# Moving the tail of a Mamba block's softplus from VectorE to GpSimd, its positive part to ScalarE

## The reference

```
xc, z = split(x @ in_w.T)
u     = silu(causal_conv(xc))
dtx, Bm, Cm = split(u @ xproj_w.T)
dt    = softplus(dtx @ dt_w.T + dt_b)
dA    = exp(dt * A);   dBu = dt * Bm * u
h_t   = dA_t * h_(t-1) + dBu_t;   y_t = h_t . C_t
out   = ((y + u * D) * silu(z)) @ out_w.T
```

## Time and profile before

| what | value |
|---|---|
| median of 3 runs (lowest, highest) | 2064.76 us (2064.29, 2065.99) |
| the profiled execution's own time | 2069.39 us |
| its span in the trace | 2067.7 us |
| VectorE busy, share of span | 1474.6 us, 71% |
| GpSimd busy | 1046.0 us, 51% |
| ScalarE busy | 860.7 us, 42% |
| TensorE matmul busy | 1518.2 us, 73% |

### The profile page before, as it was taken

How to read it: one execution, slowest core, us unless ns; L and a number is a source line. 1 busy time by engine, 2 the same in 40 slices (tenths; PEclk the granted TensorE clock), 3 DMA queues, 4 the chain that set the end, 5 groups by cost and what they waited for, 6 DMA issues and landing times. The chain is left out here.

```text
span 2067.7 us, 19480 instructions
## 1 busy us (share of the span) xinstructions
PE 1518.2 (73%) x4666; PEld 860.3 (42%) x4667; DVE 1474.6 (71%) x1703; ACT 860.7 (42%) x1848; POOL 1046.0 (51%) x531
## 2 busy tenths in 40 slices
PE   6666776786677677667767766776710999999997
PEld 3233343443344344334434433443400566666665
DVE  3699999999999999999999999999730111211111
ACT  2554554645555464555546455555300222222221
POOL 2565675666557566655756665567335111121121
PEclk8778887898888789888878987898955999999999
DMA  6312303122130312213031221303078111111111
GB/s 183 146 47 77 139 23 119 47 101 79 56 142 25 113 53 95 82 52 142 26 113 52 96 82 52 122 24 112 0 231 243 19 25 24 23 25 25 23 25 19
DMA packets 64555, 159.31 MB, mean 77 GB/s; under 512 B 10702, under 2 KB 40508, under 8 KB 63708
## 3 DMA queue, kind: packets, MB, share of 16 engines
q1 hardware_dynamic: 52716, 145.17, 20.6%
q0 software_dynamic: 11760, 13.38, 4.0%
HBM read 137.17 MB, written 21.35 MB: 77 GB/s over the span
## 5 line engine op out<-in xcount | busy, mean ns | idle before, releaser
L630 POOL TENSOR_TENSOR ring<-dtu,brep 128x1536 f32<-128x1536 f32 x192 | 660.9, 3448 | 444.7 <-DVE states L641 352.3
L653 PE MATMUL py<-ring,ident 128*128 128x384 f32 x1536 | 645.2, 573 | 128.0 <-DVE yg L670 104.3
L641 DVE TENSOR_TENSOR_SCAN states<-states,ring 128x768 f32<-128x768 f32 x384 | 673.8, 1755 | 33.9 <-ACT states L617 18.9
L653 PEld LDWEIGHTS py<-ring,ident 128*128 128x128 f32 x1536 | 336.9, 226 | 423.1 <-issue 202.0
L617 ACT ACTIVATE states<-dt_,aneg 128x376 f32<-128x376 f32 x768 | 406.1, 560 | 0.0
L643 DVE TENSOR_TENSOR ring<-states,crep 128x768 f32<-128x768 f32 x384 | 367.4, 957 | 13.2
L1271 DVE TENSOR_TENSOR hid<-act_g,gu 128x768 f32<-128x768 f32 x55 | 52.5, 954 | 425.0 <-ACT act_g L1266 425.0
L614 ACT ACTIVATE states<-zero_cols 128x16 f32<-128x16 f32 x384 | 71.3, 186 | 643.8 <-DVE ring L643 638.7
L1260 PE MATMUL gu<-w,xsT 96*128 x660 | 297.1, 600 | 7.3 <-issue 6.8
L463 PE MATMUL pf<-xT,wxz 97*128 97x384 f32 (+1 forms) x384 | 182.1, 620 | 146.8 <-ACT xT L450 55.2
L1312 POOL DMA_INDIRECT out_tokens<-ys,yidx x55 | 85.6, 1557 | 388.5 <-DVE ys L1296 379.2
(11 more groups left out here) (198 smaller groups left out, 1354.6 us busy)
## 6 DMA issues: line engine op xcount, KB each, us to landing
brep<-b_c_rows SPq DMA_DIRECT2D x64, 768.0 KB, 4.0
crep<-b_c_rows SPq DMA_DIRECT2D x64, 768.0 KB, 4.3
w<-in_w SPq DMA_DIRECT2D x8, 1152.0 KB, 34.3
slot_rows<-yg SPq DMA_DIRECT2D x1, 5390.0 KB, 21.1
xs<-slot_rows SPq DMA_DIRECT2D x55, 98.0 KB, 1.9
xe<-x_scratch SPq DMA_DIRECT2D x2, 2304.0 KB, 14.2
wd<-in_wd SPq DMA_DIRECT2D x8, 576.0 KB, 38.6
ptok<-in_p_tok SPq DMA_DIRECT2D x8, 384.0 KB, 3.7
```

The costliest lines, as they stand in the source:

```text
L630: gp.tensor_tensor(ring[:, w % NRING], dtu[:, d, o, :].unsqueeze(1).to_broadcast([128, GN, T]), brep[:, ng], ALU.mult).then_inc(dbu_ok, 1)
L641: v.tensor_tensor_scan(h_in, h_in, x_in, 0.0, ALU.mult, ALU.add).then_inc(scan_ok, 1)
L653: mm = pe.matmul(py[:, 0:T], ident[:], ring[:, w % NRING, i, :], start=(ng == 0 and i == 0), stop=False)
```

## The change

`dve_steps` is gone. The positive part max(x, 0) is a pass of its own on ScalarE (`act_relu`), and four passes run on GpSimd (`pool_steps`), the first two in one slot (`steps0`) and the last two in the next (`steps1`). Every wait on `dt` now looks at GpSimd's semaphore. To have the inputs earlier, jobs of the tables move: for dir0, `dt12_out` and `softplus` from slot 7 to 6; for dir1, `dt0` from 5 to 4, `dt0_out` and `dt12` from 7 to 5, `dt12_out` and `softplus` from 8 to 6.

```diff
-        dv = Steps(sem("dir_dve"), "conv0a conv1a conv2a conv0b conv1b conv2b m w1 r dt")
-        ds = Steps(sem("dir_act"), "silu x0 exp0 x1 exp1 ln")
+        dv = Steps(sem("dir_dve"), "conv0a conv1a conv2a conv0b conv1b conv2b")
+        dp = Steps(sem("dir_pool"), "m w1 r dt")
+        ds = Steps(sem("dir_act"), "silu x0 exp0 x1 exp1 ln relu")
...
-        def dve_steps(v, c, d):
+        def act_relu(act, c, d):
             e = 2 * c + d
-            v.wait_ge(ds.sem, ds.after("ln", e))
-            v.scalar_tensor_tensor(dt_[:, d], dtu[:, d], 0.0, dt_[:, d], ALU.max, ALU.add).then_inc(dv.sem, 1)
-
-            v.wait_ge(dv.sem, dv.after("m", e))
-            v.tensor_scalar(dtu[:, d], ea[:], 1.0, -1.0, ALU.add, ALU.add).then_inc(dv.sem, 1)
-            v.wait_ge(dv.sem, dv.after("w1", e))
-            v.tensor_tensor(ea[:], ea[:], dtu[:, d], ALU.subtract).then_inc(dv.sem, 1)
-            v.wait_ge(dv.sem, dv.after("r", e))
-            v.tensor_tensor(dt_[:, d], dt_[:, d], ea[:], ALU.add).then_inc(dv.sem, 1)
+            act.wait_ge(ds.sem, ds.after("ln", e))
+            act.activation(dtu[:, d], dtu[:, d], ACT.Relu).then_inc(ds.sem, 1)
+
+        def pool_steps(gp, c, d, part):
+
+            e = 2 * c + d
+            if part == 0:
+                gp.wait_ge(ds.sem, ds.after("relu", e))
+                gp.tensor_tensor(dt_[:, d], dtu[:, d], dt_[:, d], ALU.add).then_inc(dp.sem, 1)
+                gp.wait_ge(dp.sem, dp.after("m", e))
+                alone(gp)
+                gp.tensor_scalar(dtu[:, d], ea[:], 1.0, -1.0, ALU.add, ALU.add).then_inc(dp.sem, 1)
+            else:
+                gp.wait_ge(dp.sem, dp.after("w1", e))
+                gp.tensor_tensor(ea[:], ea[:], dtu[:, d], ALU.subtract).then_inc(dp.sem, 1)
+                gp.wait_ge(dp.sem, dp.after("r", e))
+                gp.tensor_tensor(dt_[:, d], dt_[:, d], ea[:], ALU.add).then_inc(dp.sem, 1)
...
-                2: ["bc_out"], 3: ["bc_store"], 4: ["dt0"], 5: ["dt12", "dt0_out"], 7: ["dt12_out", "softplus"],
-                8: ["z01"], 9: ["steps", "z01_out", "z2"], 10: ["z2_out"]}
+                2: ["bc_out"], 3: ["bc_store"], 4: ["dt0"], 5: ["dt12", "dt0_out"], 6: ["dt12_out", "softplus"],
+                7: ["relu", "steps0"], 8: ["steps1", "z01"], 9: ["z01_out", "z2"], 10: ["z2_out"]}
```

More of the change, by code:

```diff
@@ L468, in act_xz @@
             if tiles[0] == 0:
-                wait(act, dv.sem, dv.after("dt", e - 1))
+                wait(act, dp.sem, dp.after("dt", e - 1))
             if tiles[0] >= NC:
@@ L605, in act_decay @@
             d, o, ng = unit(w)
-            act.wait_ge(dv.sem, dv.after("dt", 2 * c + d))
+            act.wait_ge(dp.sem, dp.after("dt", 2 * c + d))
             lo = 1 if d == 0 else 0
@@ L622, in pool_input @@
             e, U = 2 * c + d, U2 * c + w
-            gp.wait_ge(dv.sem, dv.after("dt", e))
+            gp.wait_ge(dp.sem, dp.after("dt", e))
             if ng == 0:
@@ L914, in build_mamba @@
         DIR0 = {-2: ["x01"], -1: ["x01_out", "x2"], 0: ["x2_out", "conv01"], 1: ["conv2", "silu", "bc"],
-                2: ["bc_out"], 3: ["bc_store"], 4: ["dt0"], 5: ["dt12", "dt0_out"], 7: ["dt12_out", "softplus"],
-                8: ["z01"], 9: ["steps", "z01_out", "z2"], 10: ["z2_out"]}
+                2: ["bc_out"], 3: ["bc_store"], 4: ["dt0"], 5: ["dt12", "dt0_out"], 6: ["dt12_out", "softplus"],
+                7: ["relu", "steps0"], 8: ["steps1", "z01"], 9: ["z01_out", "z2"], 10: ["z2_out"]}
         DIR1 = {-2: ["x01"], -1: ["x01_out", "x2"], 0: ["x2_out", "conv01"],
-                1: ["z01", "conv2", "silu", "z01_out"], 2: ["bc", "bc_out"], 3: ["bc_store"], 5: ["dt0"],
-                7: ["dt0_out", "dt12"], 8: ["dt12_out", "softplus", "z2"], 9: ["z2_out", "steps"]}
+                1: ["z01", "conv2", "silu", "z01_out"], 2: ["bc", "bc_out"], 3: ["bc_store"], 4: ["dt0"],
+                5: ["dt0_out", "dt12"], 6: ["dt12_out", "softplus"], 7: ["relu", "steps0"], 8: ["steps1", "z2"], 9: ["z2_out"]}
         BACK = {2: ["out01"], 3: ["out01_add", "out2"], 4: ["out2_add"], 5: ["rs"], 6: ["h2"],
@@ L1072, in _ @@
                 "ahead": pool_input,
+                "steps0": lambda e, c, d: pool_steps(e, c, d, 0),
+                "steps1": lambda e, c, d: pool_steps(e, c, d, 1),
                 "h2": lambda e, c, k: None if at_end(c) else norm_h2(e, c),
@@ L1092, in _ @@
                 "dt12_out": lambda e, c, d: act_dt(e, c, d, (1, 2)),
-                "softplus": act_log,
+                "softplus": act_log, "relu": act_relu,
                 "decay": act_decay,
@@ L1110, in _ @@
                 "conv2": lambda e, c, d: dve_conv(e, c, d, (2,)),
-                "steps": dve_steps,
                 "scan": dve_scan, "gate": lambda e, c, k: dve_gate(e, c, *k),
```

## The result

| | before | after |
|---|---|---|
| median of the runs (lowest, highest) | 2065.38 us (2064.29, 2066.46), 4 runs | 2086.44 us (2084.67, 2089.72), 4 runs |
| ratio, 95% interval | 1 | 1.010 (1.0084 to 1.0116) |
| span of the profiled execution | 2067.7 us | 2084.4 us |
| VectorE, GpSimd busy | 1474.6, 1046.0 us | 1429.4, 1213.6 us |

The change makes the kernel 21 us slower; 2064 was forecast, and 2086 lies outside the range. VectorE was relieved of 45 us only, although four passes in sixteen directions (some 80 us) are gone: something else on it became longer. One execution of this whole study, of e2, took 6,226 us; it is left out, and e2's time is the median of its other three.

The account below looks back on a forecast made before the run. VectorE was taken to set the time of the Mamba stage. The terms 8.9 + 6.1 - 15.3 - 2.9 + 2.5 = -0.7 us gave 2064 us, no measurable change, range 2037 to 2077.

Parts of the forecast that it names:

- Nothing waits: Dir1 of chunks 1 to 6: GpSimd's ring inputs 10 to 12 are ready before VectorE's units need them.
- -2.54: Dir1 of each of chunks 1 to 6: -5.14 + 2.6 = -2.54 us, six times -15.3.
- -2.9: Dir1 of chunk 0: -2.9 us, with ring 11 1.4 late and unit 12's convolution absorbing 1.2 of the loss.
- Ahead of unit 0, +8.9: Before the first unit: an uncovered chain of 13.9 us in place of 4.97, so +8.9 us.
- Dir0, +6.1: Units 18 to 24, seven times: savings of 5.0 lost to three waits; 3 x 0.7 + 4 x 1.0 = +6.1 us.
- +1.0 at the loop's end: The four dir0 at the end of a loop pass: +1.0 us each, with GpSimd later out of the branch.
- The 2.6 us on the second L404 pass: Embedding, dir1 of chunks 1 to 6: the second L404 waits for GpSimd's whole first pass, +2.6 us.
- rival A: GpSimd misses the gap at L404, so the 2.6 us fall away six times: -15.6, time 2049; chance 0.22.
- L392's hold absorbing the 1.6 us: Dir1 of chunks 1 to 6: ScalarE's added 1.6 us vanish in L392's hold by GpSimd; unit 8 due as before.
- w1 at 4.2 us: GpSimd's one-input add-add pass costs 4.2 us, in proportion to L349.
- Rivals B and C: B: w1 fast, 1.5 us, time 2039, chance 0.15. C: w1 slower, 6.1 us, time 2083, chance 0.08.
- The last chunk, +2.5: Dir1 of the last chunk: no embedding covers the chain, ring inputs come late, +2.5 us.

Follow-up runs that it names:

- e2: The change for direction 0 alone, including the one ahead of unit 0; VectorE keeps direction 1 in the slots of before: 2097.50 us.
- e1: The change plus one wait: in dir1 of chunks 0 to 6 GpSimd's second pair (steps1) starts only after VectorE's x1 pass: 2061.06 us.
- e3: The change for direction 1 alone; VectorE keeps direction 0 and the one ahead of unit 0 in the slots of before: 2072.55 us.
- e6: e3 with the wait of e1 (GpSimd's second pair waits for the x1 pass): 2044.73 us.
- e7: e6 with w1 made of two cheap multiply-add passes, as in e5: 2043.37 us.
- e10: The kernel before, with the loop over chunks 2 to 6 written out: 2058.10 us.
- e12: e7 with the loop over chunks 2 to 6 written out: 2029.05 us.
- e4: The change with w1 as multiply by 1, add 0, which leaves the rounding correction out of the result: 2051.66 us.
- e5: e1 with w1 made of two passes, each a multiply by 1.0 and an add, nothing left out: 2047.13 us.
- e8: e1 with GpSimd's first pass of direction 1 also waiting for the embedding's text passes: 2060.39 us.
- e9: e2 with the loop over chunks 2 to 6 written out: 2084.67 us.
- e11: e5 with the four passes of the one direction ahead of unit 0 left on VectorE, relu on ScalarE: 2043.38 us.

## Why the prediction was wrong

**The step that failed is "Nothing waits" in dir1 of chunks 1 to 6.** The walk checked whether VectorE's units would wait for ring inputs, and there it held: ring 10 was ready before unit 9. It asked for collisions only with passes that have two SBUF inputs, and so passed over `dve_x1` (L431), which has one, and which stands in slot 8, where the change puts `steps1`. The pass is held for the whole pair, 3.8 us in each of seven chunks, some 27 us; e1 gave 25.4 of them back. With the hold the -2.54 of a chunk became +1.8 in the mean of six, and -2.9 in chunk 0 became 0.0. The Trainium skill (SBUF, State Buffer, section Who interferes with whom), which the prediction cites for the rule on two inputs, lists `tensor_scalar` in the same section among the operations that can take the shared pair of ports, under conditions on its operands. The trace agrees with that rule (4.74 us against 0.96). At the 3.8 us measured here, seven times, the sum would have been some 27 us higher, near 2091.

**Ahead of unit 0, +8.9:** right in its mechanism. From the start of relu to the end of L587 the profile shows 13.6 us against 4.9 of the four VectorE passes, +8.7. The rest of the measured 10.7 lies ahead of relu and is no part of the change: in e3, e6, e7, e10 and e12, whose code there is that of before, unit 0 also starts 0.5 to 2.2 us later.

**Dir0, +6.1:** the waits came where they were put, VectorE's on GpSimd in the last row but one and the last of these (forecast 1.9 and 3.5).

```profile
961.99 1.76 DVE L650 TENSOR_TENSOR_SCAN states<-states,ring 128x768 f32<-128x768 f32 x1 [0.96 <-ACT states L626]
975.22 1.76 DVE L650 TENSOR_TENSOR_SCAN states<-states,ring 128x768 f32<-128x768 f32 x1 [1.96 <-POOL ring L639]
983.89 1.76 DVE L650 TENSOR_TENSOR_SCAN states<-states,ring 128x768 f32<-128x768 f32 x1 [3.25 <-POOL ring L639]
```

The steps from unit 19 to unit 23 together lose 0.4 to 0.7 us in each of the seven, 0.7 was forecast. But the walk ended at unit 23, and the scan of the next unit 0 waits too, which the prediction put at nothing: at the three chunk ends without a branch that step is 1.2 to 1.3 us longer, and dir0 costs 1.6 to 1.8. The path it had overlooked runs over the load queue. SyncE, which issues the loads one after the other, comes to the last load of B (`brep`) only when GpSimd has formed the ring input of unit 23, and the first load of C (`crep`), which unit 0 needs, stands behind it. SyncE before and after, then VectorE after:

```profile
235.43 15.37 SPq L593 DMA_DIRECT2D crep<-b_c_rows  x4
```

```profile
256.61 5.27 SPq L602 DMA_DIRECT2D crep<-b_c_rows  x4
```

```profile
262.63 1.76 DVE L650 TENSOR_TENSOR_SCAN states<-states,ring 128x768 f32<-128x768 f32 x1 [1.18 <-DMA crep<-b_c_rows]
```

Before, the first of these loads was issued 9.5 us ahead of the scan of unit 23 (244.97) and landed 9.0 us before unit 0 of the next chunk; after, it is issued 0.6 us behind that scan (256.04), takes 5.9 us and lands 0.1 us before the scan that waits for it. In all seven chunk ends of the change the scan starts 0.1 us behind this landing, its ring input and its decay ready 2 us and more before it; the same holds in e1, e4, e5, e8, e9 and e11, all with dir0 on GpSimd. No run moved that load, so what it would give back isn't measured.

The +1.0 at the loop's end was mis-sized, with the wrong sign: there the step is 0.3 to 1.2 us shorter than before, and dir0 comes to between 0.0 and -1.0. What goes is the branch's stall of 2.4 us, and what stands in its place is the wait for `crep`, 1.1 to 2.2 us. The kernel moves fewer instruction packets (46 in the page, 65 before). In the kernels with the loop and 46 packets (the change, e1, e4, e5, e8, e11) no stall at the branch shows behind the landing; in those with 65 or 66 (before, e2, e3, e6, e7) it does. So dir0 measured +3.0.

**The 2.6 us on the second L404 pass:** right (L405 gained 14.4 us, 2.4 in six chunks). That GpSimd goes between two queued passes of VectorE is shown by it, so rival A is out. It was close: GpSimd's pass started 0.03 us behind the first L405 (877.76 and 877.73), 0.1 to 0.15 was forecast. e8 showed what the prediction didn't ask: taking the hold away brings nothing, as VectorE then meets the next ring input.

**L392's hold absorbing the 1.6 us:** right, L393 fell from 2.95 to 1.41.

**w1 at 4.2 us:** right (4,185 ns). Rivals B and C on its price are out. C's time, 2083, was near the result for another reason.

**The last chunk, +2.5:** +0.4 for its first half in the sum. Its ring inputs held units 10 to 12 by the forecast kind of wait, and from unit 7 to unit 12 it loses 1.9 us; 1.5 come back in units 0 to 4, which e10 shows as well (2.9) and the change doesn't touch.

## What to carry to other kernels

Before you give work to GpSimd, list every VectorE instruction that can stand beside it, those with one SBUF input too, and price each at the whole GpSimd instruction. Follow a later GpSimd result also into the load queue: a load that waits for it delays every load issued behind it. A wait that keeps the idle engine off until a short pass of the busy one is through can be worth more than the move itself. And where a pass is dear, look at its pair of operations: two cheap passes can beat a dear one.

## What the runs showed of the hardware

- A VectorE `tensor_scalar` of 192 columns with one SBUF input and per-partition scalars took 0.96 us for three alone and 4.74 us beside two GpSimd passes; it was held for both, the second starting 0.08 us behind the first.
- On GpSimd, add-add with constants took 3.6 ns an element (4,185 ns for 1,152), multiply-add 1.03 ns (1,189 ns).
- A loop branch cost VectorE 2.4 us in the kernel before, where the DMA engines were quiet, and 5.7 in e2, where they were busy. In the change, as busy (101.9%) but with no instruction packet in the gap looked at, no stall of the branch was seen. With eight VectorE instructions fewer in the loop body fewer instruction packets moved in all (46 against 65), but with four fewer not (66). Where the threshold lies was not tried.
- Of three VectorE passes queued together, GpSimd's two passes held the first for 1.77 us and the second for 2.76 us, and the third took 0.37: GpSimd's second pass came between VectorE's.
